# First norm half of an attention done in the tail of the feed-forward before it, and one stage's loads held back

## What is computed

```python
x = x + _L0_xattn_ref(_layernorm(x), ctx, ...)   # l0x, latent attention
x = x + _L0_ffn_ref(_layernorm(x), ...)          # l0f, 8 routed experts (2 a token) and one shared
x = x + _L1_xattn_ref(_layernorm(x), ctx, mask, ...)   # l1x, bounded scores, own norm behind it
x = x + _L1_ffn_ref(_layernorm(x), w1, w2)       # l1f, quantised weights and activations
x = x + _L2_xattn_ref(_layernorm(x), ctx, ...)   # l2x
x = x + _L2_ffn_ref(_layernorm(x), ...)          # l2f, gate, up, down, inner width 2048
x = x + _L3_xattn_ref(_layernorm(x), ctx, ctx, mask, ...)  # l3x, linear attention
x = x + _L3_ffn_ref(_layernorm(x), ...)          # l3f, 16 experts, 4 a token

def _layernorm(x, axis=-1, eps=1e-05):
    m = jnp.mean(x, axis=axis, keepdims=True)
    v = jnp.var(x, axis=axis, keepdims=True)
    return (x - m) / jnp.sqrt(v + eps)
```

## Time and profile before

| | us |
|---|---|
| median of three runs (lowest, highest) | 2375.53 (2372.24, 2378.52) |
| the profiled execution | 2372.35 |
| its span, first to last instruction | 2370.5 |
| TensorE, VectorE, ScalarE, GpSimd busy | 2091.8, 1085.6, 911.4, 496.1 |
| mean granted TensorE clock | 0.936 |

### The profile page before, as it was taken

The page is one execution under the profiler, slowest core; times in us unless marked ns, Lnnn a source line. Parts: engine busy times, 40 slices in busy tenths (PEclk is TensorE's granted clock), DMA queues, the critical chain, the costliest instruction groups (busy, mean ns, idle before and its releaser), DMA issues.

```text
span 2370.5 us, 39232 instructions
## 1 busy us (share of the span) xinstructions
PE 2091.8 (88%) x14719; PEld 1686.3 (71%) x14719; DVE 1085.6 (46%) x2401; ACT 911.4 (38%) x1738; POOL 496.1 (21%) x358
## 2 busy tenths in 40 slices
PE   6989999897796899986878999799987999979997
PEld 5976666687344777774567777799986999945554
DVE  4447677555113265677726666423342555511111
ACT  3246656433121354555645545322233322222221
POOL 2233232231231211100031010033312111013332
PEclk7889999999897899987989999899999999989998
DMA  3210010126324221131011000022121100379995
GB/s 108 58 39 26 13 38 1 46 74 240 103 93 122 74 71 63 68 143 40 2 64 33 16 25 2 27 76 62 45 71 43 35 26 13 106 242 328 320 322 155
DMA packets 90860, 203.68 MB, mean 86 GB/s; under 512 B 9198, under 2 KB 14418, under 8 KB 88594
## 3 DMA queue, kind: packets, MB, share of 16 engines
q1 hardware_dynamic: 80562, 174.82, 22.5%
q0 software_dynamic: 10144, 26.75, 4.3%
HBM read 183.84 MB, written 19.53 MB: 86 GB/s over the span
## 4 chain that ended last, share of the span: by engine, by line
PE 64%; DMA 11%; DVE 10%; ACT 7%; issue 5%; POOL 1%; SPq 1%; ACTq 0%; DVEq 0%; POOLq 0%
PE psum L106 14%; PE psum L107 13%; PE psum L109 13%; DMA l3f_sum_dram<-l3f_y,l3f_rows 8%; PE psum L887 3%; PE psum L3404 2%; PE psum L2637 2%; PE psum L3374 2%; PE psum L2068 1%; PE psum L2865 1%; PE psum L913 1%; DVE l2x_highest L2150 1%; PE psum L2289 1%; PE psum L3390 1%; DVE ln_stats L145 1%
## 5 line engine op out<-in xcount | busy, mean ns | idle before, releaser
L1528 PE MATMUL psum<-l3f_gate_up,l3f_x_turned 128*128 128x352 f32 x496 | 154.2, 464 | 0.8 <-ACT l3f_x_turned L1587 0.8
L1528 PEld LDWEIGHTS psum<-l3f_gate_up,l3f_x_turned 128*128 128x128 f32 x496 | 93.0, 193 | 48.1 <-issue 1.7
L3163 POOL TENSOR_TENSOR l0x_w_lo<-l0x_w_raw,l0x_w_hi 128x512 fp32r<-128x512 f32 x52 | 71.9, 1401 | 152.2 <-ACT l0x_w_hi L3416 127.8
L2109 ACT ACTIVATE l2x_probs<-psum,l2x_shift 100x361 f32<-100x361 f32 x128 | 65.0, 560 | 98.2 <-DVE l2x_shift L2154 97.0
L3518 ACT ACTIVATE l0x_probs<-l0x_probs,l0x_lowest 100x361 f32<-100x361 f32 x128 | 75.1, 588 | 59.8 <-DVE l0x_lowest L3682 59.6
L106 PE MATMUL psum<-xn_hi,l2f_w_gu_hi 128*128 128x400 f32 x256 | 90.9, 355 | 6.3 <-POOL l2f_w_gu_lo L443 2.7
L1802 POOL TENSOR_TENSOR l2x_ctx_lo<-l2x_ctx_raw,l2x_ctx_hi 128x1448 fp32r<-128x1448 f32 x8 | 26.3, 3292 | 334.5 <-ACT l2x_ctx_hi L1810 334.4
L107 PE MATMUL psum<-xn_lo,l2f_w_gu_hi 128*128 128x400 f32 x256 | 89.8, 351 | 0.0
L1503 POOL DMA_INDIRECT l3f_sum_dram<-l3f_y,l3f_rows x31 | 49.2, 1588 | 180.6 <-DMA l3f_sum_dram<-l3f_y,l3f_rows 146.0
L1554 PE MATMUL psum<-l3f_down,l3f_h_turned 128*128 128x512 f32 x186 | 85.1, 593 | 0.8 <-DVE l3f_h_turned L1619 0.8
L1613 DVE TENSOR_TENSOR l3f_h<-l3f_silu,psum 128x352 f32<-128x352 f32 x31 | 16.1, 521 | 151.8 <-ACT l3f_silu L1600 151.8
(11 more groups left out here) (533 smaller groups left out, 6190.1 us busy)
## 6 DMA issues: line engine op xcount, KB each, us to landing
l3f_gate_up<-in_slabs_dram SPq DMA_DIRECT2D x31, 1280.0 KB, 8.0
l3f_down<-in_slabs_dram SPq DMA_DIRECT2D x31, 512.0 KB, 5.5
l0x_w_raw<-in_slabs_dram SPq DMA_DIRECT2D x52, 256.0 KB, 2.7
l0f_weights<-in_slabs_dram SPq DMA_DIRECT2D x8, 1536.0 KB, 17.1
l1x_piece<-in_bit_w_dram SPq DMA_DIRECT2D x8, 1024.0 KB, 6.9
l1f_raw<-in_bit_w_dram SPq DMA_DIRECT2D x8, 1024.0 KB, 8.9
l2f_raw_gu<-in_slabs_dram SPq DMA_DIRECT2D x32, 256.0 KB, 2.7
l3f_down<-in_slabs_dram SPq DMA_DIRECT2D x31, 192.0 KB, 6.9
```

The costliest lines, as they stand in the source:

```text
L1528: mm = pe.matmul(c.psum[:, bank + x, 0:self.INNER], self.x_turned[:, t % 2, k, :], self.gate_up[:, q, at:at + self.INNER], start=k == 0, s ...
L2109: act.activation(self.probs[:, m % 2, g, :], c.psum[0:S, g, 0:C], ACT.Exp, bias=self.shift[:, g:g + 1], scale=self.SCALE).then_inc(self.s( ...
L3163: pool.tensor_tensor(self.w_lo[:, place, :], self.w_raw[:, n % 3, :], self.w_hi[:, place, :], ALU.subtract).then_inc(self.s("w_split"), 1)
```

## The change

For l1x, l2x and l3x the first norm half up to the rows is moved from the start of the attention into the tail of the feed-forward in front of it, and the attention's start is written in a new order. In the tails: VectorE runs `half_dve(.., 0)` in l0f between the additions of half 0 and the second `sums`; in l2f after the addition of unit 4; in l1f before the last batch's `add`. ScalarE runs `half_rows(.., 0)` at the end of its stage, in l0f and l2f behind a `root_table`. TensorE's `half_turn` stands before unit 4 in l0f and before unit 5 in l2f; in l1f it stays. In the attention: TensorE makes the four back transposes before its wait for `residual_ready`, then the second-half turns, then the key units; ScalarE and VectorE have the rest in the order of the diff. SyncE waits in l1x for both loads of half 1 of the routed sums (`nearly_over`) before it issues l1x's context and first six weights. No instruction's shape changes; two root tables are added.

```diff
--- before.py
+++ after.py
@@ -269,6 +269,12 @@
         n.deviation(act, b // 2)
         n.normalise(act, b)
         n.normalise(act, b + 1)
+
+
+def rows_ahead(n, act):
+
+    n.root_table(act)
+    half_rows(n, act, 0)
 
 
 def tail_pe(pe, n, unit, first_half_added):
@@ -530,7 +536,7 @@
         pe.wait_ge(c.sem(st.name + "_h_lo"), (chunk + 1) * nb)
         if isinstance(chunk, int) and chunk + 1 == st.chunks and st.index + 1 < len(c.norms):
             for u in range(2 * KD):
-                if u == KD + 2:
+                if u == KD + 1:
                     pe.wait_ge(c.sem(st.name + "_added"), chunk * KD + KD)
                     half_turn(c.norms[st.index + 1], pe, 0)
                 last_unit(u // KD, u % KD)
@@ -603,6 +609,7 @@
     for j in range(st.dn_slabs):
         ffn_high_dn(c, act, st, 0, j)
     ffn_schedule(act, st, gate_up, down)
+    rows_ahead(c.norms[st.index + 1], act)
 
 
 def ffn_row(c, dve, st, chunk, q):
@@ -682,6 +689,8 @@
                 into = c.residual[:, u % KD, a:b]
                 dve.tensor_tensor(into, into, c.psum[:, 4 + u % 4, 0:b - a], ALU.add).then_inc(
                     c.sem(st.name + "_added"), 1)
+                if u == KD:
+                    half_dve(c.norms[st.index + 1], dve, 0)
             return
         for m in range(KD):
             dve.wait_ge(c.sem(st.name + "_dn_units"), chunk * KD + m + 1)
@@ -765,6 +774,9 @@
             self.y = c.sb(second, n + "_y", [P, 2, D])
         self.x_dram = c.nc.dram_tensor(n + "_x_dram", (T + P, D), F32, kind="Internal").ap()
         self.y_dram = c.nc.dram_tensor(n + "_y_dram", (2 * T + self.TILES * P, D), F32, kind="Internal").ap()
+
+    def nearly_over(self, c, sp):
+        sp.wait_ge(self.s("sum_landed1"), 32)
 
     def prefetch(self, c, sp):
         pass
@@ -1045,6 +1057,7 @@
             if t:
                 out(t - 1)
         out(self.TILES - 1)
+        rows_ahead(c.norms[self.index + 1], act)
 
     def dve_ranking(self, c, dve):
 
@@ -1203,8 +1216,8 @@
         sums(0)
         for u in range(KD):
             add(u, 2 * KD + u)
-            if u == 0:
-                sums(1)
+        half_dve(c.norms[self.index + 1], dve, 0)
+        sums(1)
         for u in range(KD, 2 * KD):
             add(u, 2 * KD + u)
         dve.wait_ge(self.s("added"), 4 * KD)
@@ -1887,17 +1900,14 @@
 
     def pe(self, c, pe):
         n = self.norm
-        n.back(pe, 0)
-        n.back(pe, 1)
-        self.pe_keys(pe, 0, 0, 0)
-        n.back(pe, 2)
-        n.back(pe, 3)
-        self.pe_keys(pe, 0, 0, 1)
+        half_back(n, pe, 0)
         pe.wait_ge(c.sem("residual_ready"), self.index + 1)
         half_turn(n, pe, 1)
-        self.pe_keys(pe, 0, 0, 2)
+        self.pe_keys(pe, 0, 0, 0)
+        self.pe_keys(pe, 0, 0, 1)
         n.back(pe, 4)
         n.back(pe, 5)
+        self.pe_keys(pe, 0, 0, 2)
         self.pe_keys(pe, 0, 0, 3)
         n.back(pe, 6)
         n.back(pe, 7)
@@ -1941,35 +1951,24 @@
         n = self.norm
         act.wait_ge(c.sem("residual_ready"), self.index + 1)
         self.split_context_high(act, 0, 0)
-        self.split_weight_high(act, 0)
-        n.deviation(act, 0)
-        n.normalise(act, 0)
-        n.normalise(act, 1)
-        n.deviation(act, 1)
-        self.split_weight_high(act, 1)
-        n.high(act, 0)
-        n.high(act, 1)
-        n.normalise(act, 2)
-        n.normalise(act, 3)
-        self.split_weight_high(act, 2)
-        n.high(act, 2)
-        n.high(act, 3)
+        for b in range(4):
+            n.high(act, b)
+        for i in range(2):
+            self.split_weight_high(act, i)
+        for g in (2, 3):
+            n.deviation(act, g)
+            n.normalise(act, 2 * g)
+            n.normalise(act, 2 * g + 1)
+            self.split_weight_high(act, g)
         act.wait_ge(self.s("vectors_landed"), 16)
         self.act_keys(act, 0, 0, 0)
-        self.split_weight_high(act, 3)
-        n.deviation(act, 2)
-        n.normalise(act, 4)
-        n.normalise(act, 5)
-        n.deviation(act, 3)
+        self.split_weight_high(act, 4)
         self.act_keys(act, 0, 0, 1)
         n.high(act, 4)
         n.high(act, 5)
-        n.normalise(act, 6)
-        n.normalise(act, 7)
-        self.split_weight_high(act, 4)
+        self.act_keys(act, 0, 0, 2)
         n.high(act, 6)
         n.high(act, 7)
-        self.act_keys(act, 0, 0, 2)
         self.act_keys(act, 0, 0, 3)
         for i in range(5, 12):
             self.split_weight_high(act, i)
@@ -2004,15 +2003,17 @@
 
     def dve(self, c, dve):
         n = self.norm
-        half_dve(n, dve, 0)
         half_low(n, dve, 0)
+        half_dve(n, dve, 1)
         dve.wait_ge(self.s("vectors_landed"), 16)
         dve.wait_ge(self.s("bv_landed"), 16)
         self.dve_keys(dve, 0, 0, 0)
-        half_dve(n, dve, 1)
         self.dve_keys(dve, 0, 0, 1)
-        half_low(n, dve, 1)
+        n.low(dve, 4)
+        n.low(dve, 5)
         self.dve_keys(dve, 0, 0, 2)
+        n.low(dve, 6)
+        n.low(dve, 7)
         self.dve_keys(dve, 0, 0, 3)
         for m in range(3):
             self.dve_values(dve, 0, 0, m)
@@ -2945,6 +2946,7 @@
                                    c.psum[:, 4 + part, :].bitcast(BF16)[:, 0:8 * S], ACT.Copy).then_inc(
                                        self.s("inner_turned"), 1)
         self.schedule(act, first, body)
+        half_rows(c.norms[self.index + 1], act, 0)
 
     def dve(self, c, dve):
         def scales(largest, scale, step, weight, b, step_sem, name):
```

## The result

| | before | after |
|---|---|---|
| median, timed in turn on one chip (lowest, highest) | 2376.62 (2372.24, 2378.52) | 2361.81 (2357.47, 2364.19) |
| the profiled execution, its span | 2372.35, 2370.5 | 2357.47, 2355.7 |
| TensorE, ScalarE, GpSimd busy | 2091.8, 911.4, 496.1 | 2087.3, 911.5, 495.6 |
| mean granted TensorE clock | 0.936 | 0.941 |

The ratio is 0.9933, with a 95% interval of 0.9916 to 0.9949: 12 to 20 us less. The median lies 1.4 us under the forecast of 2363.2; the gain is 14.8 us by the medians and 15.9 by the ratio, where 12.3 were forecast.

What follows compares the result with a forecast made beforehand. Each attention's head was taken as one chain through the norm that delays the value products. Gains of 7.4 + 1.6 + 3.3 = 12.3 us from the median 2375.5 gave 2363.2 us, range 2357 to 2371.

Steps and rivals of the forecast that it cites:

- The head: Attention start, from the release (VectorE's last residual addition) to the first value product: one chain through the norm, 22.7 us in l1x.
- J2: Place from l1f to l2x: release 2.2 us late, value products 1.6 us sooner.
- J3: Place from l2f to l3x: release 1.75 us late, value products 3.3 us sooner.
- V: Start of the value products, waiting for the eighth split weight; all behind it follows by the same steps before and after.
- J1: Place from l0f to l1x: release 2.75 us early, 7.4 us gained (6.4 if the hold does nothing, 8.3 at best).
- the landing of half 0: In l0f's tail, the routed sums' first half lands at 740.4 instead of 741.4 us; T is their first load's issue.
- the 0.8 for slow key units: In the heads of l2x and l3x, key units at TensorE's low clock cost 0.8 us each place.
- The two locks: In the new heads, two small VectorE shifts wait for GpSimd over shared ports; without this the head is 1.3 us shorter.
- 1, the low clock filling a head: TensorE at 1.2 GHz through all key units: head 29.6 instead of 22.7; one place 2370, all three 2382; chance 0.12.
- 2, the head keeps its length: Something other than the norm orders the weights; late releases stay, 1.95 us later, 2377.5; chance 0.06.
- 3, the low clock past V: With all heads low, value units stay slow too: 2.4 us a unit, 14 in all, 2396; chance 0.03.
- 4, the held context late: l1x's held context load takes its 20.0 us again, so l1x starts 11 us later: 2374; chance 0.05.

Runs made afterwards that it cites:

- before, again: The kernel before, unchanged, run against itself under another label: ratio 0.9999 (0.9987 to 1.0011).
- only l3x: The kernel before with only l3x's new start and l2f's new tail, without SyncE's new wait: 0.9986 (0.9977 to 0.9995), 3.3 us.
- one scalar operand: The changed kernel with the norm's small shift as two instructions, each with one tensor and one scalar operand: 0.9925 (0.9911 to 0.9939).
- no hold, again: The changed kernel without SyncE's new wait for the routed sums, run a second time: 0.9936 (0.9916 to 0.9956).
- the hold alone: The kernel before with only SyncE's new wait for the routed sums added: 0.9981 (0.9970 to 0.9993).
- old norm, earlier weights: The kernel before with ScalarE's weight copies 4 to 7 put into its waits for the second norm half: 2360.37 us, 0.9940 (0.9920 to 0.9959).

## Why the prediction was right, and where not

**The mechanism held.** The head was one chain through ScalarE's order; it was worth 22.7 us in the new order by the prediction, and 22.74, 22.75 and 22.72 were measured. These heads count from the context copy; from the release, as the prediction counts, J2's is 23.7 (24.3 forecast) and J3's 22.8 (23.5 forecast). That V waited for the copies because of their place in the order is shown by two experiments: copies 4 to 7 moved alone shorten the old heads, 27.2 to 28.4, to 24.2 to 24.7, and copies 2 to 7 moved shorten the new ones to 17.6, 18.3 and 18.6. The norm's own work counts as well: with the copies out of the way, some 6 to 7 us a head still lie between the old place of the norm and the new one (where copies 2 and 3 moved as well).

**J1 was over-sized: 7.4 forecast, 5.2 at V in the two profiles, 6.3 at Q over all runs without another edit at J1.** The term that failed is the landing of half 0. I let it gain 1.0 us from the hold, 10.95 behind T; it came at 13.21, 2.3 later. So the release came 0.7 us earlier behind T than before, where 2.75 was forecast; the rest of the 5.2 is the head. From S on all was right: S to R 18.07 against 18.25 forecast, the head to 0.04. I had the share (10 of 16 engines) and the rate (168 to 213 GB/s measured beside my 176), but worked as if half 0 were done when half the bytes are. The trace shows loads that end unevenly, with a share that falls from 0.17 on. Whether this uneven end is also what delays half 0 was not measured. Nor is the hold clearly what made S late: without it T-S was 11.5 to 12.6 in the old order and 12.35 and 13.67 in two runs of the new; with it, 12.5 to 13.2 (means 12.2 without it, over seven runs, and 13.0 with it, over six; the ranges overlap). The forecast's 10.95 lies under all of them. My bound for "the hold does nothing", 11.95, came from one execution and was too narrow.

**In the changed kernel the hold does nothing for the time that can be told**, by 0.9933 against 0.9936, and 0.9851 against 0.9862 (intervals overlap in both). Its cost was rightly put at nothing. The ring order of the Trainium skill ("DMA: Bandwidth & Descriptors", "Queues, rings and completion order") is in agreement: loads issued behind the sums did not delay them by an amount that these runs can tell.

**J2: 1.6 forecast, 1.5 measured to Q, but by two errors.** O to V gained 2.4 in the two profiles, because the 0.8 for slow key units was charged and did not fall due: the head is 22.75 without it, at a mean clock of 0.80. Behind V the sum said "the same steps before and after". In the changed kernel the first value unit ran wholly at the low clock, in the old one only partly. The old kernel's l2x (against the row at 1197.05 above):

```profile
1211.09:1216.09 5.00, 4.41 (x12) 3.20 (x12) 0.55 (x1) 2.04 (x2) 4.92 (x5) 0.70 0.56 218
```

A clock of 0.70 against 0.50, so V to Q took 1.1 us more. The two errors all but cancelled, so that the hit at J2 is luck. The second is part of the spread of executions: l2x in the old order had 30.6 us from V to Q in four runs and 31.6 in one (before, again), in the new order 31.6 to 31.8 in each. V was the wrong place to end the sum.

**J3: 3.3 forecast, 3.5 measured to Q, 4.3 at V in the two profiles.** R comes 1.4 late where 1.75 was forecast, from U 11.40 against 10.01; the slow units were charged here too, and this execution had none. In three others with the new order they fell due: the clock dropped to 0.50 ahead of the first key unit, and the head was 23.1 (only l3x), 23.3 (one scalar operand) and 23.4 (no hold, again), 0.4 to 0.7 longer. The heads after and in the last of these, columns as in the earlier trace rows:

```profile
1744.40:1767.12 22.72, 12.41 (x84) 11.35 (x85) 10.93 (x24) 15.57 (x31) 13.37 (x10) 0.97 0.35 101
```

```profile
1750.80:1774.12 23.32, 14.69 (x84) 13.73 (x85) 10.95 (x24) 15.61 (x30) 13.39 (x10) 0.80 0.35 99
```

So the charge of 0.8 had its reason, and that the profiled execution went without it at J3 was luck.

**The two locks** behaved as forecast: 0.50 and 0.96 us, each ending with a difference of GpSimd's. The rule was cited from "SBUF — State Buffer", "Who interferes with whom", of the Trainium skill; the trace agrees, and the form with one tensor and a scalar operand escapes. But the 1.3 us that I put on the locks gave 1.05 in one head, 0.55 in the second and less than 0.1 in the third at an equal clock, less 0.34 in each tail, and no gain in the total that can be told.

**The rivals.** 1, the low clock filling a head: at J1 and J2 the mean clock of the new head was 0.80 (in the old heads 0.85 and 0.75), and both took 22.7 us; the longest new head, at J3 in another run, took 23.4; refuted, with 0.7 us of its kind at most. 2, the head keeps its length: refuted by the heads of 22.7. 3, the low clock past V: its mechanism was there in the small, in the first value unit alone, for about 1 us at J2; the second unit is at 0.95 or more, so its price of 14 never came. 4, the held context late: its load was issued at 746.8, and the copy at 756.52 waited for VectorE; refuted.

**What stays open.** The marks give 10.8 us for the changed kernel, the medians 14.8 and the ratio 15.9; for all but two of the other changed kernels, too, the ratio gives 3 to 10 us more than the marks, for the hold alone 4.5 against nothing, and for the same kernel again nothing. T lay at 726.1 on average over the eleven changed kernels of the table and at 728.5 in the two of the old one, though nothing but an added table load in ScalarE's idle time stands ahead of it, and in four of the eleven not even that. In the two profiled executions the 14.8 us of the spans are 4.3 us ahead of T and 10.9 in the marks, less 0.3 between and behind them. So there the surplus lies ahead of T; whether it does in the other executions, and why, stays open. Between the places (Q to O, Q to U, Q to the end) the sum was 1416 to 1427 us without a pattern. So the forecast of 2363.2 came nearer to 2361.8 than its parts deserve, and that is luck: J1 was 1.1 too much, and some 4 us came from elsewhere.

## What to carry to other kernels

When several engines serve one head, look for the instruction that the last wait traces back to and ask what stands ahead of it in its own engine's order. Here moving four copies into waits of the same engine, a move of a few lines, gained as much as moving half a norm across a stage boundary. Both together, with two more copies moved, gained 35 us, more than the sum of the two: 31 by the marks, where each alone gave 11.

End the sum not at the first product that comes sooner but at the first one behind it that runs at full clock: with a shorter pause ahead of a dense stretch up to 2.4 us more were gained behind it. And a load's landing read from one execution is known to no better than a microsecond or two; bound it by several.

## What the runs showed of the hardware

- TensorE's granted clock over the first 5 us of the values, by the idle time ahead of them: 0.50 to 0.71 behind 6.05 us (old order), 0.66, 0.50 and 0.50 behind 5.5 us (after), 0.66 three times behind 2.27 us (old norm, earlier weights), and behind 1.84 us 1.00 in five of nine starts and 0.66 in four, among them l1x and l3x of the run with earlier weights and no hold. The mean clock of the head does not tell which: 0.79 to 0.83 ahead of the five, 0.83 to 1.00 ahead of the four, but 0.79 ahead of the three behind 2.27 us.
- A VectorE instruction on 100 x 2 elements with two tensor operands from SBUF took 0.16 us alone and up to 1.04 beside a GpSimd difference; two on 100 x 1 with one tensor and a scalar operand took 0.34 together in either case. So the second form pays only beside GpSimd's work.
- The four loads of the sums, at 0.65 to 0.67 of the DMA engines, did not move faster when the queue behind them was empty, and ended with some 2 us at 0.17 and less (0.12 and 0.11 at 746 and 748 in the hold-only run).
- The same kernel run against itself gave 0.9999 (0.9987 to 1.0011), while single stretches of it without any edit differ by 1 us, and the time up to T by 2.
